# Feed-forward of the second layer: row normalisation on GpSimd, closing sum split between ScalarE and GpSimd

## What is computed

```
def _mx_dequant(t):                       # blocks of 32 along the row
    max_abs = jnp.max(jnp.abs(blocks), axis=-1)
    scales = jnp.maximum(max_abs / 448.0, 1e-30)
    q = (blocks / scales[..., None]).astype(jnp.float8_e4m3fn).astype(jnp.float32)
    return (q * scales[..., None]).reshape(rows, feat)

gate = _mx_dequant(x2d) @ _mx_dequant(gate_w).T      # x2d = layernorm(x), 256 -> 1024
up   = _mx_dequant(x2d) @ _mx_dequant(up_w).T
h    = silu(gate) * up
out  = _mx_dequant(h) @ _mx_dequant(down_w).T        # 1024 -> 256
x    = x + tanh(g_ffn[1]) * out
```

## Time and profile before

| | us |
|---|---|
| median of 3 runs | 512.68 (511.4 to 513.83) |
| the profiled execution, its own time | 514.03 |
| its span in the profile | 512.3 |
| DVE busy in the span | 351.4 (69%) |
| PE busy | 406.5 (79%) |
| POOL busy | 247.5 (48%) |
| ACT busy | 181.4 (35%) |
| 403.00 to 512.30: DVE, PE, POOL, ACT busy | 93.82, 94.11, 50.02, 20.86 |

### The profile page before, as it was taken

The page is one execution under the profiler, slowest core; times in us unless marked ns, Lnnn a source line. Parts: engine busy times, 40 slices in busy tenths (PEclk is TensorE's granted clock), DMA queues, the critical chain, the costliest instruction groups (busy, mean ns, idle before and its releaser), DMA issues.

```text
span 512.3 us, 8514 instructions
## 1 busy us (share of the span) xinstructions
PE 406.5 (79%) x2839; PEld 289.6 (57%) x2839; DVE 351.4 (69%) x840; ACT 181.4 (35%) x416; POOL 247.5 (48%) x347
## 2 busy tenths in 40 slices
PE   0476788778677899999699678768887899988884
PEld 0265666666446566677477456556665455555543
DVE  0568886656986455589577326857857699999992
ACT  0353465445301454444244242325354122222210
POOL 2356565423227577777441265866212245555451
PEclk9987798879959899999899699979997999999998
DMA  7999961112923597668954342433110000000000
GB/s 222 266 216 271 242 237 52 52 52 59 170 41 100 130 297 224 173 173 181 161 150 142 118 137 80 146 87 118 57 42 1 0 1 12 10 10 12 11 10 22
DMA packets 72314, 57.42 MB, mean 112 GB/s; under 512 B 38864, under 2 KB 64592, under 8 KB 72272
## 3 DMA queue, kind: packets, MB, share of 16 engines
q1 hardware_dynamic: 60880, 37.23, 27.9%
q0 software_dynamic: 4608, 12.59, 10.8%
q10 hardware_dynamic: 6784, 7.05, 4.1%
HBM read 42.18 MB, written 14.68 MB: 111 GB/s over the span
## 4 chain that ended last, share of the span: by engine, by line
PE 47%; issue 16%; DVE 15%; POOL 10%; ACT 3%; DMA 3%; ACTq 3%; another core or an unknown queue 2%; POOLq 0%; DVEq 0%
PE psum L1214 9%; PE psum L1380 6%; PE psum L1401 4%; PE psum L1237 3%; PE psum L1398 3%; POOL arena_dn L628 3%; PE psum L1371 3%; POOL mx_w L631 2%; PE psum L1224 2%; PE psum L1283 2%; DMA bias_bc<-_xattn_norm_k_img_w_dram 2%; PE psum L1229 2%; PE psum L1281 2%; PE psum L1470 2%
## 5 line engine op out<-in xcount | busy, mean ns | idle before, releaser
L542 POOL DMA_INDIRECT shared<-h_dram,tok_u x64 | 66.9, 1046 | 49.9 <-PE psum L1214 22.3
L1501 PE MATMUL psum<-arena_dn 128*128 128x512 f32 x128 | 57.1, 598 | 3.2 <-ACT arena_dn L785 3.2
L628 POOL TENSOR_TENSOR arena_dn<-arena_dn 128x512 f32<-128x512 f32 x16 | 20.3, 1271 | 45.6 <-DVE arena_dn L1047 45.6
L1501 PEld LDWEIGHTS psum<-arena_dn 128*128 128x128 f32 x128 | 23.7, 190 | 31.2 <-issue 26.3
L566 POOL DMA_INDIRECT arena_up<-ys_dram,slot_u x32 | 31.4, 981 | 14.1 <-issue 14.1
L1078 DVE TENSOR_TENSOR h1T<-psum,h1T 128x128 f32<-128x128 f32 x32 | 9.3, 292 | 40.0 <-ACT h1T L733 37.4
L1214 PE MATMUL psum<-ident,mx_w 128*128 128x128 f32 x128 | 23.3, 312 | 16.2 <-POOL mx_w L631 8.9
L1214 PE MATMUL psum<-ident,arena_dn 128*128 128x128 f32 x96 | 18.3, 310 | 21.8 <-DVE arena_dn L878 19.3
L1214 PE MATMUL psum<-ident,arena_up 128*128 128x128 f32 x144 | 25.0, 292 | 12.4 <-DVE arena_up L1105 2.9
L1214 PEld LDWEIGHTS psum<-ident,mx_w 128*128 128x128 f32 x128 | 16.8, 158 | 27.1 <-POOL mx_w L631 10.9
L1596 PE MATMUL psum<-arena_dn,mx_w 128*128 128x256 f32 x128 | 30.1, 390 | 0.4 <-ACT mx_w L795 0.3
(11 more groups left out here) (226 smaller groups left out, 1065.4 us busy)
## 6 DMA issues: line engine op xcount, KB each, us to landing
ys_dram<-stage SPq DMA_DIRECT2D x32, 256.0 KB
arena_up<-in_L_ffn_wg_dram SPq DMA_DIRECT2D x8, 512.0 KB, 8.3
arena_up<-in_L_ffn_wu_dram SPq DMA_DIRECT2D x8, 512.0 KB, 7.4
h1T<-in_L_ffn_wd_dram SPq DMA_DIRECT2D x64, 64.0 KB
arena_dn<-in_L_ffn_wd_dram SPq DMA_DIRECT2D x3, 1024.0 KB, 11.5
va_dram<-stage ACTq DMA_DIRECT2D x8, 256.0 KB, 3.7
kT_dram<-stage ACTq DMA_DIRECT2D x8, 256.0 KB, 4.6
arena_up<-kT_dram SPq DMA_DIRECT2D x8, 256.0 KB, 2.7
```

Source lines behind the costliest of these rows:

```text
L542: pool.indirect_dma_start(out=xg[n % 4][:, b, :], out_offset=None, in_=h1_dram[:, :], in_offset=bass.IndirectOffsetOnAxis(ap=tok_u[:, 2 * ...
L628: pool.tensor_tensor(haF[h], haF[h], heF[h], ALU.subtract).then_inc(sem("hint"), 1)
L1501: ins = pe.matmul(bank[2 * part + h][:, :], xTF[n % 2][:, c, :], mx_gu[:, c, lo:lo + HW], start=(c == 0), stop=(c == C - 1))
```

## The change

Three things move. The normalisation L1128 leaves DVE: POOL makes it right behind inv_sqrt, in the same step, into the same two buffers. The closing sum of tiles 0 to 6 is split: ACT multiplies bank 4 by the gate into a new SBUF tile dFs (two of them, taken from free space), and POOL adds that to x_res. The last tile's closing sum stays on DVE. PE's down product now waits for ACT's copy (dFs) and no longer for the sum (x4). Besides, the pads' own semaphore padE is merged into pad, with the wait moved from 4 to 8, and a count on slot_u that nobody waits for is dropped.

```diff
@@ POOL, ffn_pool
                     inv_sqrt(rstd[:, b:b + 1], mv[:, b, 1:2], LN_EPS, "mvF", i.n + 1, "rstdF")
+                    pool.wait_ge(sem("rstdF"), i.n + 1)
+                    pool.tensor_scalar(xnF[b], x_res[:, i.n, :], mv[:, b, 0:1], rstd[:, b:b + 1],
+                                       ALU.subtract, ALU.mult).then_inc(sem("xnF"), 1)
                 i = at(1)
 ...
+                i = at(3)
+                if i is not None and i.n < T - 1:
+                    pool.wait_ge(sem("dFs"), i.n + 1)
+                    pool.tensor_tensor(x_res[:, i.n, :], x_res[:, i.n, :], dFs[i.n % 2], ALU.add).then_inc(sem("x4"), 1)
                 i = at(2)
@@ ACT
+            def closing(n):
+                act.wait_ge(sem("dF"), n + 1)
+                reach(act, sem("x4"), n - 1)
+                act.activation(dFs[n % 2], bank[4][:, 0:D], ACT.Copy, scale=tg[:, GF1:GF1 + 1]).then_inc(sem("dFs"), 1)
 ...
                 if k < T:
                     row_out(k)
+                if k > 1:
+                    closing(k - 2)
+                if k < T:
                     for h in range(2):
                         gate(k, h)
@@ DVE, row_quant and the end of the loop
-                dve.wait_ge(sem("rstdF"), n + 1)
-                chain(dve.tensor_scalar(xnF[s], x_res[:, n, :], mv[:, s, 0:1], rstd[:, s:s + 1],
-                                        ALU.subtract, ALU.mult), "r")
+                dve.wait_ge(sem("xnF"), n + 1)
 ...
-                n = k - 3
-                dve.wait_ge(sem("dF"), n + 1)
-                dve.scalar_tensor_tensor(x_res[:, n, :], bank[4][:, 0:D], tg[:, GF1:GF1 + 1], x_res[:, n, :],
-                                         ALU.mult, ALU.add).then_inc(sem("x4"), 1)
+            n = T - 1
+            (the same sum, once)
@@ PE, ahead of the down product
-                reach(pe, sem("x4"), n)
+                reach(pe, sem("dFs"), n)
```

More of the change, by code:

```diff
@@ L315, in build_program @@
         haF = [take(HW) for _ in range(2)]
+        dFs = [take(D) for _ in range(2)]
         take = carver(mx_w)
@@ L550, in _ @@
             for b in range(2):
-                pool.memset(qn[b][:, :, HD:HP], 0.0).then_inc(sem("padE"), 1)
-                pool.memset(qb[b][:, D:D + 1], (D * RMS_EPS) ** 0.5).then_inc(sem("padE"), 1)
+                pool.memset(qn[b][:, :, HD:HP], 0.0).then_inc(sem("pad"), 1)
+                pool.memset(qb[b][:, D:D + 1], (D * RMS_EPS) ** 0.5).then_inc(sem("pad"), 1)
             for k in range(ahead[0], NWC):
@@ L976, in _ @@
             chain(dve.tensor_tensor(slotf, slotf, pick0, ALU.add), "r")
-            dve.tensor_copy(slot_u[:, :], slotf).then_inc(sem("slot_u"), 1)
+            dve.tensor_copy(slot_u[:, :], slotf)
             chain(dve.tensor_copy(slot_i, slotf), "r")
@@ L1086, in _ @@
             dve.wait_ge(sem("gu"), NG // 2)
-            dve.wait_ge(sem("padE"), 4)
+            dve.wait_ge(sem("pad"), 8)
             dve.wait_ge(sem("gob"), 4)
@@ L1202, in _ @@
                         half_quant(k - 2, h)
-                n = k - 3
-                dve.wait_ge(sem("dF"), n + 1)
-                dve.scalar_tensor_tensor(x_res[:, n, :], bank[4][:, 0:D], tg[:, GF1:GF1 + 1], x_res[:, n, :],
-                                         ALU.mult, ALU.add).then_inc(sem("x4"), 1)
+            n = T - 1
+            dve.wait_ge(sem("dF"), n + 1)
+            dve.scalar_tensor_tensor(x_res[:, n, :], bank[4][:, 0:D], tg[:, GF1:GF1 + 1], x_res[:, n, :],
+                                     ALU.mult, ALU.add).then_inc(sem("x4"), 1)
         @block.tensor
```

## The result

The changed kernel takes 518.77 us (median of 4 runs, 517.39 to 520.35) against 512.77 (4 runs, 511.40 to 513.83) of the kernel before in the same series: ratio 1.012, 95% interval 1.0078 to 1.0161. It is slower, as forecast, but 3.0 us above the forecast of 515.8 and 0.8 above the upper end of the range.

A forecast was written before the change was run, and what follows sets the result against it. The feed-forward was taken as bound by DVE operations waiting for POOL at the shared port. Six tiles' 1.8 plus the tail's 1.3 gave +3.1 us: 517.1 profiled, median 515.8, range 510.4 to 518.0.

The forecast's parts named there:

- DVE bounds only through the port: Feed-forward tiles: DVE looks busiest, but some of its operations wait for POOL at the shared port; 13.2 us a tile.
- all of them 0.40, which I take: Normalisation of 256 columns on POOL: length taken as 0.40 us, bounded by 0.29 below and 0.73 above.
- The tile laid out by hand: One feed-forward tile, instruction by instruction: 13.63 us instead of 13.20, +0.43; +0.30 taken for each of six tiles.
- The other branch: Same tile if the normalisation takes 0.5 us or more: L1041 slips in ahead of L622; tile 13.38, +0.18.
- The tail, +1.3: End of the feed-forward: tile 6's addition waits for ACT ahead of tile 7's halves in POOL's queue; +1.3 us.
- 1.8 + 1.3 = +3.1 us: Whole span: six tile lengths plus the tail, added to the profiled execution of 514.03, giving 517.1.
- From the profiled execution to the median: Profiled execution lies 1.35 us over the median of 512.68, so the forecast median is 515.8.
- (a): Feed-forward: work leaves DVE for good, added POOL work finds gaps at the port; 2.3 to 3.6 us off, 509.8; 17%.
- (b): Feed-forward: tile stays at 13.2 because POOL's L631 fixes L1043; the tail costs 0.6 to 1.3; 513.6; 27%.
- (c): Feed-forward: port saturated, every added POOL length paid; 0.83 a tile, 5.0 in six, 1.3 in the tail; 519.0; 8%.
- No time saved at the end of L1043: Second half of a feed-forward tile: listed as a sign that the forecast is right, though the layout had 0.44 left.
- A POOL normalisation of over 1 us would make the sum too small: Normalisation on POOL: a warning sign that a length over 1 us means more than the forecast +3.1 us.

The follow-up runs named there:

- norm_act: Kernel before with the normalisation of tiles 3 to 7 on ScalarE, closing sum still on DVE; 495.10 us against 498.41, ratio 0.9954.
- norm_only: Changed kernel with the closing sum kept on DVE, so only the normalisation moves to POOL; 514.36 us, ratio 1.012 to the kernel before.
- close_only: Changed kernel with the normalisation kept on DVE, so only the closing sum is split; 514.59 us, ratio 1.0061 to the kernel before.
- norm_copy: Changed kernel with POOL's normalisation replaced by a copy of the same 256 columns; 514.64 us, ratio 1.0134 to the kernel before.
- close6_dve: Changed kernel with tile 6's closing sum on DVE as well as tile 7's; 517.64 us, ratio 1.0161 to the kernel before.
- add_1col: Changed kernel with POOL's addition cut to one column, queue place and waits kept; 513.66 us, ratio 1.0047 to the kernel before.
- warm_after: Changed kernel with 13 calls of filler products on PE ahead of the waits for tile 7's halves; 513.73 us, ratio 1.0166 to the kernel before.
- add_behind: Changed kernel with POOL's addition behind both halves of the later tile in its step; 499.44 us against 498.41 before, ratio 1.011.
- sem_only: Kernel before with only the padding's semaphore merged and the count on slot_u dropped; 510.92 us against 510.82, ratio 1.0032.

## Why the prediction was wrong

The direction held, and that DVE and POOL share a port; the sizes did not, and in two places a right total hides wrong steps. Two steps failed: the length given to the normalisation on POOL (0.40 for 1.36 us), through which the six tiles cost 2.57 instead of 1.8, and the end behind POOL's last instruction, put at nothing, where the traces differ by 1.00. The 3.0 us by which the median missed are 0.8 in the tiles, -0.1 in the tail, 1.0 behind it, and 1.2 that are not in the feed-forward and stay open. Point by point:

- *DVE bounds only through the port.* Right. Two instructions left DVE and its busy time rose. norm_act shows what taking the normalisation off is worth when the port is left alone, norm_only and close_only what it is worth when it isn't.
- *The normalisation on POOL, "all of them 0.40, which I take".* Wrong, and the first of the two steps. I scaled a one-column row and a half-width copy to an operation that no row showed, with 0.73 as the upper bound. It takes 1.36 in the kernel and 1.22 alone. norm_copy puts the price of this one number at 1.37 us in six tiles. By the rule that I had quoted, the Trainium skill's one cycle an element for a short body (GPSIMD Engine Reference, § 3.1), the estimate was 0.41, and it erred with me; the measured 1.22 decides.
- *The tile laid out by hand.* With 0.40 it gave +0.43, with 0.5 or more +0.18; the runs say +0.15 for the copy of 0.40 (norm_copy) and +0.49 for 1.36. The layout for 0.40 has the right waits and ends 0.30 late: in norm_copy POOL's next instruction starts 0.04 before the recorded end of the copy and of the addition, where I had put 0.08 after it. The other branch has a right step and a wrong price: L1041 does slip in ahead of the old L622, but only after a wait for L619 (0.47 for 0.18), and L1043 then waits for L622 (0.89 for 0.69). The mean that I took, +0.30, lay 0.19 under the measured steady tile, and six of them gave 1.8 for 2.57, near the top of its own bounds (1.1 to 2.6). That this term is only 0.77 short is luck: the length cost 1.37, and the layout had charged 0.6 too much without it (80.31 - 79.11 = 1.20 measured, 1.8 forecast). The sixth tile had no normalisation behind it and cost 0.02; I had charged it like the others.
- *The tail, +1.3.* Right in size: +1.24, and the last L639 ended 13.56 after the last half of tile 6 where my layout had 13.61. That the addition's place in the queue causes it is shown by close6_dve (-1.73) and add_1col. The order at the port is not the one laid out: there the addition waited for L1045, and L631 for the last L1047; in the trace L1061 waits for the addition (0.99) and the last L1063 for L639 (1.42). That two orders end within 0.05 us of each other is luck.
- *The sum, "1.8 + 1.3 = +3.1 us".* The second step: it ends at POOL's last instruction, and puts what comes behind at nothing without a reason. There the two traces differ by +1.00, and that is the granted clock (warm_after). Whether the change adds anything to it stays open: kernels that leave PE's last waits as they were show anything from 8.12 to 9.36 us there (add_behind, close6_dve), and the kernel before, at 8.27, lies near the low end.
- *From the profiled execution to the median.* Put in place of 3.1, the +4.80 of the feed-forward give 517.5, inside the range. The medians are 6.0 us apart, and the interval of the ratio reaches from 4.0 to 8.3. The last 1.2 us are not in the feed-forward. Times resolve no more than that: norm_only's median is 1.7 us over the kernel before with a feed-forward 0.3 longer, close_only's 1.9 with one 5.05 longer. sem_only excludes the small edits as a cost above 0.7%. What else differs ahead of the feed-forward, where the instructions are the same, stays open; so the ratios of the other experiments are not used to weigh reasons of a us or two.
- *Rivals.* (a) and (b) fell on the tiles: none of 12.7 to 12.9, and only the sixth at 13.2. (c), 519.0, is nearest to the measured time, but not for its reason: it charged 0.83 a tile (5.0 in six) and the tiles gave 2.57. Its tiles would have been 14.0. Only in the tail did POOL take the port ahead of L1061 to L1063 each time, as it had it.
- *What would show it.* L1056 directly behind L1139, the stretched L1063, less idle time on POOL with tiles of 13.67, and the start of tile 7's first half at 500.79 (after 499.5) came as written. "No time saved at the end of L1043" did not: 0.45 was saved, as my own layout had it (0.44). L636 of the first half came behind L1063 as said, but it was L1063 that the addition held, not the reverse: 0.72 for the addition, 1.13 for L1063. "A POOL normalisation of over 1 us would make the sum too small" is what happened.

## What to carry to other kernels

Before moving elementwise work from VectorE to GpSimd, find who shares the port with whom in the trace: here an engine with half its time idle had no free place for an addition of 0.72 us in either of two tried, while the normalisation, moved to ScalarE instead, shortened the tile to 0.04 us over PE's own length. Price an operation only by a row of the same form on the same engine; a copy is no measure for a two-operation tensor_scalar. End the sum at the end of the span, not at the last instruction that the change touches; where TensorE idles for some us near the end, the product behind it may run at either clock, so compare several traces before the difference is put down to the change.

## What the runs showed of the hardware

- POOL's tensor_scalar with two operations in f32: 1.22 us on 256 columns, 0.79 on 128, 0.58 on 64; with constants 1.07. A copy of 256 columns takes 0.40, an addition of two tiles 0.72. The Trainium skill (GPSIMD Engine Reference, § 4.1) calls one-input elementwise work on GpSimd roughly line-rate; the copy fits that (0.40, less the 0.19 of a one-column row, is 0.8 ns a column, where this form takes 3.4 ns from 128 to 256 columns), this form doesn't.
- ScalarE makes the same normalisation (bias and scale per row) in 0.60 us, the mean of the five in the loop of norm_act.
- Behind one idle stretch of 4.0 us the last turning took 1.11 to 1.12 and the last down product 4.52 to 5.72 us in seven traces, after filler products 0.60 to 0.66 and 3.62 in three.
- Filler products that overrun the gap cost what they win: 7.07 us of them in a gap of 4.0 left the end at 9.49 us, 0.27 over norm_act's.
